# Causal attention: where groups are loaded, scored ahead and given their maxima, and when the dispatch buffers are zeroed

## What is computed

```python
def _L1_xattn_ref(q, latent_kv, Wq, Wkv_expand, Wout):
    B, S, H, NH, L = (2, 512, 512, 16, 128)
    HD = H // NH
    qp = q @ Wq.T
    kv = latent_kv @ Wkv_expand.T
    k, v = jnp.split(kv, 2, axis=-1)
    # heads: (b, NH, s, HD)
    scores = jnp.einsum('bhqd,bhkd->bhqk', qh, kh) * inv_sqrt_d
    scores = jnp.where(causal, scores, jnp.finfo(scores.dtype).min)
    attn = jax.nn.softmax(scores, axis=-1)
    out = jnp.einsum('bhqk,bhkd->bhqd', attn, vh)
    return out.transpose(0, 2, 1, 3).reshape(b, sq, H) @ Wout.T

x = x + _L1_xattn_ref(_layernorm(x, axis=-1), ctx_512, L1_xattn_Wq, L1_xattn_Wkv_expand, L1_xattn_Wout)
```

## Time and profile before

| | us |
|---|---|
| median of 3 runs | 3918.41 |
| lowest and highest | 3912.83, 3923.32 |
| the profiled execution | 3951.42 |
| its span, first to last instruction | 3949.5 |
| PE busy in the span | 3208.8 (81%) |
| DVE, ACT, POOL busy | 2297.0, 1816.2, 532.6 |

### The profile page before, as it was taken

The page is one execution under the profiler, slowest core; times in us unless marked ns, Lnnn a source line. Parts: engine busy times, 40 slices in busy tenths (PEclk is TensorE's granted clock), DMA queues, the critical chain, the costliest instruction groups (busy, mean ns, idle before and its releaser), DMA issues. The chain is left out here.

```text
span 3949.5 us, 60203 instructions
## 1 busy us (share of the span) xinstructions
PE 3208.8 (81%) x15894; PEld 2206.5 (56%) x15894; DVE 2297.0 (58%) x3966; ACT 1816.2 (46%) x3138; POOL 532.6 (13%) x1022
## 2 busy tenths in 40 slices
PE   4349997678776299966889779999989698979998
PEld 2137775444444188843333347788877333336886
DVE  6964445344434333347889544566646788965555
ACT  5643334233332145534677623366633377773433
POOL 2420000022231300021000130022211000010000
PEclk7669998777778599986999779999999699999999
DMA  4334445943321233334222242367644322212223
GB/s 142 139 103 138 136 140 175 360 126 90 95 55 54 98 101 112 107 111 156 52 51 52 68 161 93 111 240 242 226 139 138 128 52 54 54 29 79 94 93 117
DMA packets 242233, 464.89 MB, mean 118 GB/s; under 512 B 57572, under 2 KB 74084, under 8 KB 241554
## 3 DMA queue, kind: packets, MB, share of 16 engines
q1 hardware_dynamic: 200528, 330.01, 27.2%
q0 software_dynamic: 22480, 96.23, 7.1%
q10 hardware_dynamic: 19090, 37.23, 2.5%
HBM read 346.93 MB, written 113.77 MB: 117 GB/s over the span
## 5 line engine op out<-in xcount | busy, mean ns | idle before, releaser
L1698 DVE TENSOR_REDUCE at_maxima<-psum 128x1 f32<-128x512 f32 (+1 forms) x768 | 613.5, 860 | 51.1 <-PE psum L1599 48.7
L1677 ACT ACTIVATE at_probs<-psum 128x512 f32<-128x512 f32 x1024 | 529.4, 604 | 247.5 <-PE psum L1615 246.2
L1615 PE MATMUL psum<-at_qT,at_kT 50*128 50x512 f32 x1024 | 389.7, 463 | 91.7 <-ACT at_probs L1677 49.3
L585 PE MATMUL psum<-f_xT_hi,ffn_w_hi 128*128 x1024 | 406.0, 396 | 9.7 <-DVE f_xT_lo L313 2.3
L585 PE MATMUL psum<-f_xT_lo,ffn_w_hi 128*128 x1024 | 405.3, 396 | 0.0
L1599 PE MATMUL psum<-at_kT,at_qT 48*128 48x512 f32 x1024 | 387.3, 481 | 13.6 <-DVE at_maxima L1698 11.5
L1615 PEld LDWEIGHTS psum<-at_qT,at_kT 50*128 50x128 f32 x1024 | 175.6, 193 | 388.9 <-ACT at_probs L1677 276.9
L1628 PE MATMUL psum<-at_probs,at_vals 128*32 128x512 f32 x2048 | 285.7, 631 | 0.0
L602 PE MATMUL psum<-ffn_w_hi,ffn_hid_hi 128*128 128x512 f32 x768 | 269.2, 391 | 1.3 <-ACT ffn_hid_hi L648 1.3
L393 PE MATMUL psum<-ident,n_normed 128*128 128x128 f32 x512 | 103.4, 372 | 199.4 <-ACT n_normed L356 158.7
L490 ACT ACTIVATE ffn_w_hi<-ffn_w_raw 128x512 fp32r<-128x512 f32 x262 | 161.4, 633 | 156.8 <-PE psum L607 99.7
(11 more groups left out here) (381 smaller groups left out, 6892.4 us busy)
## 6 DMA issues: line engine op xcount, KB each, us to landing
ffn_w_raw<-in_stream SPq DMA_DIRECT2D x262, 256.0 KB, 2.9
ffn_w_hi<-quantized SPq DMA_DIRECT2D x66, 512.0 KB, 3.5
ffn_w_hi<-quantized SPq DMA_DIRECT2D x65, 256.0 KB, 3.2
at_qT<-q_hi SPq DMA_DIRECT2D x256, 64.0 KB, 2.2
ffn2a_w_raw<-in_shared2a SPq DMA_DIRECT2D x26, 512.0 KB
ffn2b_w_raw<-in_shared2b SPq DMA_DIRECT2D x26, 512.0 KB
qz_raw<-in_stream SPq DMA_DIRECT2D x17, 768.0 KB, 4.3
quantized<-qz_quant POOLq DMA_DIRECT2D x16, 768.0 KB, 3.5
```

Source lines behind the costliest of these rows:

```text
L585: mm = pe.matmul(hid_ps[h][s][0:n, :], wt[s][:, w], xt[:, c, bass.ds(b * S, S)], start=(c == 0 and i == 0), stop=(c == DC - 1 and i == len ...
L1615: pe.matmul(scoreT[turn_of(n)][:, :], kT[r][half(h % 2, USED + 2), t * P:(t + 1) * P], qT[r][half(h % 2, USED + 2), h // 2, :], start=True ...
L1677: act.activation(probs[n % RING][:, :], scoreT[turn_of(n)][:, :], ACT.Exp, scale=factor).then_inc(exped, 1)
L1698: dve.tensor_reduce(maxima[:, h:h + banks, t], scores, AX.X, ALU.max).then_inc(maxed, 1)
```

## The change

It has five parts, all for the causal attention:

1. Eight stacks in place of four (`SLOTS`), and no wait of SP before a load. VectorE sets rows of eight `kT`.
2. Plain scores run three groups ahead (`LEAD`): three groups before the slots, and those of s + 3 in slot s. Maxima are split, sent and put two groups ahead, s + 2 in slot s.
3. On SP the put stands ahead of the load, and the load is that of group s + 4.
4. Values are stored unpadded, 2 KB for a token. Their load is taken from SP and given to ScalarE: two DMAs for a group, one for each head, in pieces of 32 values (128 bytes), at the end of a slot. The padding is set once by GpSimd in the eight `vals`. PE waits for the values with a semaphore of their own, `v_landed`, ahead of the first result of a group.
5. The zeros are written in 32 pieces, at the end of each slot, by two DMAs of ScalarE (64 rows of `gathered1`, 192 of `gathered2`), in runs of 1 KB.

```diff
@@ stage_causal_inputs
-        v_out = [sb(f"v{s}", [P, D // HEAD1, 2 * HEAD1]) for s in range(2)]
+        v_out = [sb(f"v{s}", [P, D]) for s in range(2)]
...
-                pool.memset(v_out[s][:, :, HEAD1:2 * HEAD1], 0.0).then_inc(padded, 1)
...
-                pool.memset(v_out[s][:, :, HEAD1:HEAD1 + 1], 1.0).then_inc(padded, 1)
...
-                sp.dma_start(values[i * P:(i + 1) * P, :], v_out[i % 2][:, :, :].rearrange("p h o -> p (h o)")).then_inc(v_kept[i % 2], DMA)
+                sp.dma_start(values[i * P:(i + 1) * P, :], v_out[i % 2][:, :]).then_inc(v_kept[i % 2], DMA)
...
-            sp.wait_ge(padded, 4)
...
-                    act.activation(v_out[i % 2][:, :, 0:HEAD1], kv_ps[1][:, :].rearrange("p (h d) -> p h d", d=HEAD1), ACT.Copy).then_inc(v_made, 1)
+                    act.activation(v_out[i % 2][:, :], kv_ps[1][:, :], ACT.Copy).then_inc(v_made, 1)
@@ stage_attend_causal
-    RING, SLOTS = PAIRS, 4
+    RING, SLOTS, LEAD = PAIRS, 8, 3
...
-    ROUNDS = (GROUPS - 1 - SLOTS) // ROUND
-    LOADS, PUTS = 2 * PARTS + 1, H
+    ROUNDS = (GROUPS - 1 - LEAD - 1) // ROUND
+    LOADS, PUTS = 2 * PARTS, H
...
+    VALUE_LOADS = H
...
+            for r in range(SLOTS):
+                pool.memset(vals[r][:, :, :, HD:OW], 0.0).then_inc(cleared, 1)
...
+            for r in range(SLOTS):
+                pool.memset(vals[r][:, :, :, HD:HD + 1], 1.0).then_inc(consts, 1)
...
-                rows = values[tokens, n * P:(n + 1) * P].rearrange("(t p) f -> p t f", p=P)
-                sp.dma_start(vals[r][:, :, :, :].rearrange("p t h o -> p t (h o)"), rows).then_inc(landed[r], DMA)
...
-            for g in range(SLOTS - 1):
+            for g in range(LEAD + 1):
                 load(g, 0)
-            send_max(0, 0)
-            put_max(0, 0)
+            for g in range(2):
+                send_max(g, g)
+                put_max(g, g)
 
             def slot(s, place, j, ahead):
-                if ahead >= 1:
-                    send_max(place + 1, s + 1)
-                if ahead >= 3:
-                    if not is_first(s):
-                        sp.wait_ge(valued, RING + PAIRS * s)
-                    load(place + 3, j)
-                if ahead >= 1:
-                    put_max(place + 1, s + 1)
+                if ahead >= 2:
+                    send_max(place + 2, s + 2)
+                    put_max(place + 2, s + 2)
+                if ahead > LEAD:
+                    load(place + LEAD + 1, j)
 
             all_slots(sp, slot)
-            sp.wait_ge(slots_cleared, 3 * DMA)
+            sp.wait_ge(slots_cleared, (2 * GROUPS + 1) * DMA)
...
-            def results(g, place, t):
...
+            def results(g, place, j, t):
...
+                if t == 0:
+                    pe.wait_ge(v_landed[place % SLOTS], VALUE_LOADS * DMA * (use(place, j) + 1))
...
-            for g in range(2):
+            for g in range(LEAD):
                 for n in range(PAIRS):
                     scores(g, g, 0, n)
...
-                    if ahead >= 2:
-                        scores(s + 2, place + 2, j, n)
+                    if ahead >= LEAD:
+                        scores(s + LEAD, place + LEAD, j, n)
...
         def _(act):
-            clear_slots(act)
             act.sem_inc(exped, 2)
+            act.wait_ge(consts, CONSTS)
+
+            def load_values(place, j):
+
+                b, n = batch_piece(place, j)
+                for h in range(H):
+                    rows = values[bass.ds(b * S, S), (n * H + h) * HD:(n * H + h + 1) * HD].rearrange("(t p) d -> p t d", p=P)
+                    act.dma_start(vals[place % SLOTS][:, :, h, 0:HD], rows).then_inc(v_landed[place % SLOTS], DMA)
+
+            for g in range(LEAD + 1):
+                load_values(g, 0)
...
+                if ahead > LEAD:
+                    load_values(place + LEAD + 1, j)
+                clear_slots(act, s)
...
-            for n in range(PAIRS):
-                maximum(0, n)
-            split_maxima(0, 0)
-            for n in range(PAIRS):
-                maximum(1, n)
+            for g in range(LEAD):
+                for n in range(PAIRS):
+                    maximum(g, n)
+                if g < 2:
+                    split_maxima(g, g)
 
             def slot(s, place, j, ahead):
-                if ahead >= 1:
-                    split_maxima(s + 1, place + 1)
+                if ahead >= 2:
+                    split_maxima(s + 2, place + 2)
                 for n in range(PAIRS):
-                    if ahead >= 2:
-                        maximum(s + 2, n)
+                    if ahead >= LEAD:
+                        maximum(s + LEAD, n)
@@ build_program
-        def clear_slots(act):
-
-            for name in ("gathered1", "gathered2"):
-                rows = scratch[name].rearrange("(t p) d -> p t d", p=P)
-                act.dma_start(rows, zeros[:, :].rearrange("p (o d) -> p o d", o=1).to_broadcast([P, rows.shape[1], D])).then_inc(slots_cleared, DMA)
-            act.dma_start(scratch["answers1"][N:N + 1, :], zeros[0:1, :]).then_inc(slots_cleared, DMA)
+        def clear_slots(act, s):
+
+            for name, count in (("gathered1", N // GROUPS), ("gathered2", (BLOCKS2 + 1) * BLOCK2 // GROUPS)):
+                part = count * D // P
+                src = zeros[:, 0:D // 2].rearrange("p (o d) -> p o d", o=1).to_broadcast([P, 2 * part // D, D // 2])
+                dst = scratch[name][bass.ds(s * count, count), :].rearrange("r d -> (r d)").rearrange("(p c d) -> p c d", p=P, d=D // 2)
+                act.dma_start(dst, src).then_inc(slots_cleared, DMA)
+            if isinstance(s, int) and s == 0:
+                act.dma_start(scratch["answers1"][N:N + 1, :], zeros[0:1, :]).then_inc(slots_cleared, DMA)
```

More of the change, by code:

```diff
@@ L925, in stage_causal_inputs @@
         k_out = [[sb(f"k_{part}{s}", [P, S], F32R) for part in ("hi", "lo")] for s in range(2)]
[L926 removed]
+        v_out = [sb(f"v{s}", [P, D]) for s in range(2)]
         q_ps, kv_ps = room.banks[4:6], room.banks[6:8]
[L928 to L929 removed]
+        (q_landed, kv_landed, wq_hi, wq_lo, wkv_hi, wkv_lo, c_hi, c_lo, q_product, q_hi, q_lo, k_product, k_hi, k_lo, v_product, v_made) = k.sems(
+            ctx, nm, "q_landed kv_landed wq_hi wq_lo wkv_hi wkv_lo c_hi c_lo q_product q_hi q_lo k_product k_hi k_lo v_product v_made")
         c_landed, q_kept, k_kept, v_kept, c_kept = ([k.sems(ctx, nm, f"{n}{s}")[0] for s in range(2)]
                                                    for n in ("c_landed", "q_kept", "k_kept", "v_kept", "c_kept"))
[L933 to L939 removed]
         def pieces(dst, c, b):
@@ L1177, in stage_attend_causal @@
         turn = room.tiles(4 + (RES + 1) % TURNS)
-        landed, put = ([k.sems(ctx, nm, f"{n}{r}")[0] for r in range(SLOTS)] for n in ("landed", "put"))
+        landed, put, v_landed = ([k.sems(ctx, nm, f"{n}{r}")[0] for r in range(SLOTS)] for n in ("landed", "put", "v_landed"))
         (keys_cleared, cleared, consts, scored, maxed, max_split, max_turned, max_out, scoredT, exped, selected, valued, res_moved, turned_res,
@@ L1184, in all_slots @@
         def all_slots(engine, slot):
-            slot(0, 0, 0, SLOTS)
+            slot(0, 0, 0, LEAD + 1)
             with engine.Fori(0, ROUNDS) as j:
                 for r in range(ROUND):
-                    slot(ROUND * j + r + 1, r + 1, j, SLOTS)
+                    slot(ROUND * j + r + 1, r + 1, j, LEAD + 1)
             for s in range(ROUND * ROUNDS + 1, GROUPS):
@@ L1241, in load @@
                         sp.dma_start(tile[i * HD:(i + 1) * HD, :, :].bitcast(F32), rows).then_inc(landed[r], DMA)
-                rows = values[tokens, n * P:(n + 1) * P].rearrange("(t p) f -> p t f", p=P)
-                sp.dma_start(vals[r][:, :, :, :].rearrange("p t h o -> p t (h o)"), rows).then_inc(landed[r], DMA)
             def send_max(place, g):
                 sp.wait_ge(max_turned, g + 1)
-                sp.dma_start(tops[place % SLOTS, :, :], across[place % 2][:, :]).then_inc(max_out, DMA)
+                sp.dma_start(tops[place % 4, :, :], across[place % 2][:, :]).then_inc(max_out, DMA)
             def put_max(place, g):
@@ L1253, in put_max @@
                 sp.wait_ge(max_out, DMA * (g + 1))
-                rows = tops[r, :, :].rearrange("(b h o t) i -> h o t b i", b=TB, h=2 * H, o=2)
+                rows = tops[place % 4, :, :].rearrange("(b h o t) i -> h o t b i", b=TB, h=2 * H, o=2)
                 for h in range(H):
@@ L1303, in scores_T @@
                           start=True, stop=True).then_inc(scoredT, 1)
-            def results(g, place, t):
-                if t == 0 and not is_first(g):
-                    pe.wait_ge(res_moved, g)
+            def results(g, place, j, t):
+                if t == 0:
+                    pe.wait_ge(v_landed[place % SLOTS], VALUE_LOADS * DMA * (use(place, j) + 1))
+                    if not is_first(g):
+                        pe.wait_ge(res_moved, g)
                 for h in range(H):
@@ L1329, in slot @@
```

(16 more changed lines are left out.)

13 lines of the change are left out of this document (3 added, 10 removed).

## The result

The changed kernel takes 3857.0 us (median of 4 runs, 3852.3 to 3860.9), the kernel before 3918.9 (3912.8 to 3923.3): a ratio of 0.984, interval 0.9825 to 0.986. The change gave 62 us where 37 were expected.

A forecast was written before the change was run, and what follows sets the result against it. PE was taken to be held by waits for the maxima and the low clock that goes with them. Prologue -20.4, slots -22.3 + 5.5, ends 0 made -37.2: 3918.4 - 37.2 = 3881.2 us, range 3836 to 3908.

The forecast's parts named there:

- Prologue: Ahead of the slots: with the zeros gone from there, slot 0 starts at about 775.5, 20.4 us earlier.
- The exchange of waits: In the slots: PE's wait for the maxima goes, but little is gained, as the load takes its place.
- The chain C: In the slots: from the last plain score to the landing of the load of s + 4, 11.1 us (10.4 to 13.3).
- W, the slow slot's work: PE's work in the second of two slots, at the low clock: 11.5 us, 0.6 either way.
- the prediction's own formula: Two slots together take C + W - 0.4: 11.1 + 11.5 - 0.4 = 22.2 us, so a slot 11.1 instead of 11.47.
- The regular alternation: In the slots: a full-clock slot ends in a gap of 2.8 to 3.5 us, and a slow slot follows.
- The end: Behind the 29 slots: three slots without plain scores and the tail take 20.2 us; the last zeros add 1 (0 to 2).
- the slots net of the lost one: The slots save 22.3 us, less 5.5 for the slot that lost its plain scores.
- The one microsecond allowed for the stage before: In the stage before, which PE bounds, less is stored: -1 us (0 to -2).
- Rival A: In the slots: delay spreads evenly, gaps about 1.2 us, clock stays up, a slot 9.2 us, total 3826; chance 0.12.
- Rival B: In the slots: SP's issues stretch to 1.2 us, the load bounds outright, a slot 13.35 us, +65, 3946; chance 0.06.
- Rival C: In the slots: ScalarE's four issues take 1.2 us each, 4.8 a slot, +22, 3903; chance 0.10.

The follow-up runs named there:

- both moves: Changed kernel with SP's load ahead of send and put, and ScalarE's four DMA issues ahead of its last exponential: 3807.24 us, ratio 0.964 to the kernel before.

## Why the prediction was right, and where it was off

**Prologue: right.** Forecast 20.4 us, measured 19.9 (slot 0 at 776.0 and not 775.5). SP's first load came at 756.6 (755.9), its issues mostly came 0.47 us apart, as forecast, and PE started at 762.6 (762.0). With the zeros whole at the start, slot 0 fell back to 801.0, so this gain is the zeros' alone. They gave 24.5 us in the kernel before; the rest of the change, with its four more memsets and its third group, takes some 5 back.

**The exchange of waits: right.** The maxima's waits went, waits for the keys came. They came in ten slots of 29 and not in every second one. Putting ahead of the load in the kernel before, and loading ahead of the put in the changed one, each moved the wait as forecast.

**The chain C, from the last plain score to the landing of the load: right.** Forecast 11.1 us; in the pair above 905.44 to 906.98 is 1.54, to the put 1.90, to the first load 1.49, to the last of its six issues 2.30, and to PE's start 3.70. The sum is 10.93. Over the ten waits of over 2 us it is 10.5 to 11.9, and once 13.4, with a mean of 11.2.

**W, the slow slot's work: the step that was off.** The prediction set it at 11.5 us, the work of the slow slot in rows 4, because it expected a gap of 2.8 to 3.5 us, "as long as the one that precedes slow slots now". In the pair it is 9.97. By the prediction's own formula two slots then take 10.93 + 9.97 - 0.4 = 20.5, measured 20.6, where 22.2 was forecast. Over the 29 slots 321.9 us were forecast and 303.3 measured. The forecast has 14.5 x (6.8 + 11.5) = 265.4 us of work in them and 56.5 idle; measured are 252.4 and 50.9. So 13 of the 18.6 us are work.

Part of this is known. The full-clock slot was longer than the 7.7 us assumed (8.27, as ScalarE's issues cost PE 1.23 us and not up to 0.9), and so the gap was 2.4 us and not 2.8 to 3.5. Longer gaps had more work behind them on the whole: with the doubled put gaps of 3.5 to 5.1 us have 10.9 to 11.6 us. But W is not a function of the gap either. In the changed kernel seven gaps of 2.1 to 2.6 us all have 9.96 to 10.01 us, two longer ones (2.7 and 2.9) only 8.41, and one of 4.9 has 11.01. With the zeros whole, two equal gaps have 9.20 and 12.27. W was taken as a constant from one slot; it moved between 8.4 and 12.3 us, and what sets it in a given slot stays open. So does the reason why eight slots without such a gap were slow. The regular alternation on which the sum rests held for about half of the slots, so that the slots' mean came near the forecast is partly luck.

**The end.** 23.6 us behind the 29 slots, 20.2 forecast; in part because the low clock is still on when it begins (0.93). In the same kernel on another chip it took 22.0, nearly all at full clock.

Together: -20.4 + 0.5 for the prologue, -16.8 (the slots net of the lost one) - 18.6, and + 3.4 for the end, which is the 51.9 us measured. The one microsecond allowed for the stage before is not to be seen: PE's busy time there is 79.25 us, before 79.18.

**The other 10 us.** The median fell by 61.9, this stage by 51.9. Of the 24 us by which the time lies below the forecast, 15 are thus this stage's and 10 lie outside it, where the prediction had no term; that they are on the side of a gain is luck. The second layer's shared attention, which the change doesn't touch, took less time in the profile of the changed kernel (columns as in rows 1; the first row is the kernel before):

```profile
1822.20:2131.70 309.50, 272.87 (x1628) 111.09 (x1628) 270.35 (x426) 207.85 (x403) 22.53 (x46) 0.93 0.24 64
```

```profile
1769.10:2069.90 300.80, 269.10 (x1620) 108.83 (x1618) 270.79 (x426) 205.87 (x400) 21.75 (x45) 0.94 0.24 68
```

Counted from VectorE's first result there to its 25th, it is 293.0 us before and 285.8 in the changed kernel; 291.8 and 293.3 in the two kernels built on the one before, 282.7 to 286.9 in the ten built on the changed one. So it goes with the change and not with the run, but I have no cause for it, and no run tried one. Behind it the last results of that stage take 75 to 87 us, and the rest of the program varies by some 28 us, whatever the kernel. The profiled execution of the kernel before lay at the long end of both, which is probably most of its 33 us above the median. To read the change from the two spans (3949.5 and 3853.5) would give 96 us.

**The rivals.** Rival A (the clock stays up) needed gaps near 1.2 us in every slot. Only the kernel with the load ahead has them, from ScalarE: its slots take 9.43 us, where A has 9.2, but its clock is 0.85, as ten slots fell to the low one. The kernel with both moves has 0.90. So A's premise that 1.2 us is safe was too good. That the slow clock comes back behind each wait for DMA, as the Trainium skill has it (page "TensorE: Matmul & The Clock Gate", section "HAM oscillation"), is what the pairs of slots above show at 2.38, 3.92 and 5.46 us of wait. But four waits of 2.3 us with the load one group earlier show that it is not so each time. Rival B (SP's issues at 1.2 us) didn't happen. But what it describes is real: with 1.3 us more in SP's chain the change loses 32 us of its gain. Rival C (ScalarE binds) didn't happen either: its issues took 0.39 and 0.54 us each, 2.3 us in the slot of the pair, not 4.8.

## What to carry to other kernels

When PE's work alternates between a gap and the low clock, don't take the slow part's length from one slot. Here the same work took from 8.4 to 12.3 us, and both 9.2 and 12.3 behind gaps of one length, so read it from all slots and give it a range of its own. A microsecond on the chain that causes the gap can count more than double (1.3 us more in the chain, 3.1 us more in a pair, in the one run that tried it). Write out the one queue's whole round (send, wait for what was sent, put, load) and compare it with the slot. What stood in front of the next load set the pace here, and more lead for the load only renamed the wait. And judge such edits in pairs: ScalarE's issues moved earlier cost 27 us alone and gave some 36 us (1.25 a slot) with the load moved ahead. Last, take both ends of a stage at the same event: the last matmul and the next stage's first DMA are 1 us apart here.

## What the runs showed of the hardware

- The low clock can follow a wait of PE, but the wait's length doesn't fix how much work falls to it: 8.41 us of work in a slot behind 2.87 us, 9.97 behind 2.38, 9.20 and 12.27 behind 3.84 and 3.85, 11.54 behind 3.92 (all of it takes 6.8 to 7.0 at full clock). Ten of 29 slots had it with no wait over 1.6 us (once 2.1), and four waits of 2.3 us in another run were not followed by it.
- Landing depends on what another queue issues in the same few microseconds. The last of six loads of 128 KB took 3.7 us until PE ran with ScalarE's four DMAs issued 3 to 5 us ahead of the first (and the next four 1 to 3 us behind the last), and 5.8 with them between its issues; the medians to landing are 3.6 and 4.6.
- A transfer of 16 KB behind six loads on SP's queue, with ScalarE's four DMAs issued beside them, took 5.7 us until SP could go on, and 1.44 with no load ahead of it.
- A DMA piece of 128 bytes took 13.7 ns and one of 512 bytes 30.6 ns in two kernels that are alike otherwise.
- Traffic isn't priced by its bytes alone. The same zeros in pieces cost 0.7 us a slot in the kernel before, where the maxima were needed at once, and nothing (-0.3) in the changed one.
